# Node stage of a graph network: where GpSimd makes two low parts, and which engine casts what

## What is computed

```
h   = layernorm(x)
agg = segment_sum(relu([h[src], edge_attr] @ W1.T + b1) @ W2.T + b2, dst)
gi  = agg @ W_ih.T + b_ih ;  gh = h @ W_hh.T + b_hh
r   = sigmoid(i_r + h_r) ; z = sigmoid(i_z + h_z) ; n = tanh(i_n + r * h_n)
h_new = (1 - z) * n + z * h
x1  = x + h + batchnorm(h_new)
h2  = layernorm(x1)
top 2 of 8 gate logits -> softmax -> comb (8 numbers a node, 2 not zero)
out = x1 + sum_e comb_e * (relu(h2 @ W1_e + b1_e) @ W2_e + b2_e) + 0.5 * shared(h2)
```

## Time and profile before

| | |
|---|---|
| median of three runs | 1423.47 us |
| profiled execution | 1422.28 us, span 1420.5 us |
| TensorE busy | 1356.3 us (95%) |
| weight load busy | 1088.8 us (77%) |
| VectorE | 1030.6 us (73%) |
| GpSimd | 827.6 us (58%) |
| ScalarE | 738.2 us (52%) |
| mean granted TensorE clock | 0.991 of full speed |
| DMA | 179.57 MB, 126 GB/s over the span |

### The profile page before, as it was taken

One profiled execution on the slowest core, in us unless ns is written; L12 is line 12 of the kernel. 1 busy time (PEld: TensorE's weight loads), 2 busy tenths in 40 slices (PEclk: granted clock), 3 DMA queues, 4 the chain that ended last, 5 costly groups with the idle time before them and its releaser, 6 DMA issues.

```text
span 1420.5 us, 22825 instructions
## 1 busy us (share of the span) xinstructions
PE 1356.3 (95%) x6398; PEld 1088.8 (77%) x6398; DVE 1030.6 (73%) x2194; ACT 738.2 (52%) x1665; POOL 827.6 (58%) x1119
## 2 busy tenths in 40 slices
PE   4889999999889999999999999999999999999996
PEld 3668888887668777877787778777777777777774
DVE  3586444233478888888888888888888888888885
ACT  3431323212466566656665666566666666666552
POOL 3210242103477777777777777777777777777771
PEclk9999999999989999999999999999999999999997
DMA  8222534246423333333333333333333333333330
GB/s 311 69 68 88 185 135 144 90 152 244 163 97 126 119 132 112 127 116 133 113 129 112 133 118 125 111 133 118 125 111 133 119 124 112 131 122 122 114 109 30
DMA packets 62863, 179.57 MB, mean 126 GB/s; under 512 B 9328, under 2 KB 9968, under 8 KB 62704
## 3 DMA queue, kind: packets, MB, share of 16 engines
q1 hardware_dynamic: 46912, 99.20, 20.4%
q0 software_dynamic: 15920, 79.97, 16.4%
HBM read 141.86 MB, written 37.29 MB: 126 GB/s over the span
## 4 chain that ended last, share of the span: by engine, by line
PE 89%; DVE 4%; issue 2%; DMA 1%; ACT 1%; POOL 1%; POOLq 0%; SPq 0%; DVEq 0%; ACTq 0%
PE bank L1547 45%; PE bank L1584 9%; PE bank L1214 8%; PE bank L1594 8%; PE bank L526 6%; PE bank L1166 5%; PE bank L1184 4%; PE bank L1197 3%; PE bank L1596 1%; POOL whh_lo_raw L766 1%; PE bank L1148 1%; DVE st_e L890 1%; DMA late_out<-gates_in,carry_at 1%; DMA whh_lo_raw<-in_whh_t 0%; DVE found L957 0%
## 5 line engine op out<-in xcount | busy, mean ns | idle before, releaser
L1547 PE MATMUL bank<-whh_hi,x_hi 128*128 128x512 f32 x948 | 382.5, 403 | 10.8 <-DVE x L1493 10.5
L1547 PE MATMUL bank<-whh_hi,x_lo 128*128 128x512 f32 x948 | 375.3, 396 | 0.0
L1547 PE MATMUL bank<-whh_lo,x_hi 128*128 128x512 f32 x948 | 375.2, 396 | 0.0
L1547 PEld LDWEIGHTS bank<-whh_hi,x_hi 128*128 128x128 f32 x948 | 178.5, 188 | 51.6 <-DVE x L1493 10.9
L1547 PEld LDWEIGHTS bank<-whh_hi,x_lo 128*128 128x128 f32 x948 | 178.4, 188 | 43.5
L1547 PEld LDWEIGHTS bank<-whh_lo,x_hi 128*128 128x128 f32 x948 | 178.7, 189 | 39.1
L1295 POOL TENSOR_TENSOR rstd<-var_eps,minus_half 128x1 f32<-128x1 f32 x158 | 90.6, 574 | 149.5 <-DVE var_eps L479 149.5
L1346 POOL TENSOR_TENSOR h_n<-h,n_gate 128x512 f32<-128x512 f32 x79 | 103.9, 1315 | 58.6 <-ACT n_gate L1402 58.6
L504 ACT ACTIVATE h<-xt,shift,rstd 128x512 f32<-128x512 f32 x79 | 64.5, 816 | 134.1 <-POOL one_rstd L1301 134.1
L1286 POOL DMA_INDIRECT gates<-gates_in,slot_at x79 | 85.3, 1079 | 60.0 <-issue 45.7
L1342 POOL TENSOR_TENSOR n_pre<-r_hn,gates 128x512 f32<-128x512 f32 x79 | 102.6, 1299 | 13.4 <-POOL r_hn L1338 13.2
(11 more groups left out here) (184 smaller groups left out, 3148.6 us busy)
## 6 DMA issues: line engine op xcount, KB each, us to landing
xt<-in_x SPq DMA_DIRECT2D x79, 256.0 KB, 2.9
x_lo_raw<-in_x_cols SPq DMA_DIRECT2D x79, 256.0 KB, 2.7
out<-y SPq DMA_DIRECT2D x79, 256.0 KB, 2.0
gates_in<-g_out SPq DMA_DIRECT2D x16, 768.0 KB, 4.0
wih_lo_raw<-in_wih_t SPq DMA_DIRECT2D x4, 768.0 KB, 15.7
whh_rows<-in_whh SPq DMA_DIRECT2D x4, 768.0 KB
whh_lo_raw<-in_whh_t SPq DMA_DIRECT2D x4, 768.0 KB, 7.5
gates_in<-late_out SPq DMA_DIRECT2D x6, 256.0 KB, 6.8
```

Of the source, the lines that this page charges most:

```text
L1547: last = pe.matmul(to[0:R, :], a[:, s, k * R:(k + 1) * R], w[:, k, q * D:(q + 1) * D], start=n == 0, stop=n == 3 * DK - 1)
```

## The change

Three engines' orders change in the node stage, and one instruction goes from VectorE to ScalarE. On GpSimd the extras' low part of tile t-2 goes from behind the slot copy to right behind the second norm, and `x_low` of tile t+1 from behind `x_h_b` to between n_pre and the wait for tanh. On ScalarE the extras' cast goes from behind the r gate's sigmoid to ahead of the second norm's rows. The cast of the expert numbers leaves VectorE, and ScalarE does it after its wait for `top_i_done`, ahead of the shared expert's relu, with one more wait for the weight products of the tile before.

```diff
 # GpSimd
                 if p.has(-1):
                     norm(p, -1, 2)
+                if p.has(-2):
+                    s = p.slot(-2)
+                    pool.wait_ge(extra_hi_done, t - 1)
+                    pool.tensor_tensor(hid[:, s, HE + 2 * V:HE + 3 * V], extra[:, :], hid[:, s, HE:HE + V],
+                                       ALU.subtract).then_inc(extra_lo_done, 1)
                 if p.has(1):
...
-                if p.has(1) and not p.early(1):
-                    x_low(pool, p)
                 if p.has(2) and not p.early(2):
                     pool.wait_ge(gates_loaded[p.slot(0)], 16 * (p.turn(0) + 1))
                     slots(p, 2)
-                if p.has(-2):
-                    s = p.slot(-2)
-                    pool.wait_ge(extra_hi_done, t - 1)
-                    pool.tensor_tensor(hid[:, s, HE + 2 * V:HE + 3 * V], extra[:, :], hid[:, s, HE:HE + V],
-                                       ALU.subtract).then_inc(extra_lo_done, 1)
...
                     pool.tensor_tensor(n_pre[:, :], r_hn[:, :], gates[:, s, 2 * D:G3], ALU.add).then_inc(n_pre_done, 1)
+                if p.has(1) and not p.early(1):
+                    x_low(pool, p)
+                if p.has(0):
+                    s = p.slot(0)
                     pool.wait_ge(n_done, t + 1)
 # ScalarE
                 if p.has(2) and not p.early(2):
                     first_norm(act, p)
+                if p.has(-2):
+                    s = p.slot(-2)
+                    act.wait_ge(comb_done, t - 1)
+                    wait_from(act, hid_turned, t - 3)
+                    act.activation(hid[:, s, HE:HE + 2 * V].bitcast(F32R).rearrange("p (q v) -> p q v", q=2),
+                                   extra[:, :].unsqueeze(1).broadcast_to((R, 2, V)), ACT.Copy).then_inc(extra_hi_done, 1)
                 if p.has(-1):
...
-                if p.has(-2):
-                    s = p.slot(-2)
-                    act.wait_ge(comb_done, t - 1)
-                    wait_from(act, hid_turned, t - 3)
-                    act.activation(hid[:, s, HE:HE + 2 * V].bitcast(F32R).rearrange("p (q v) -> p q v", q=2),
-                                   extra[:, :].unsqueeze(1).broadcast_to((R, 2, V)), ACT.Copy).then_inc(extra_hi_done, 1)
...
                     act.wait_ge(top_i_done, t)
+                    wait_from(act, comb2_done, t - 1)
+                    act.activation(top_f[:, :], top_i[:, 0:2], ACT.Copy).then_inc(top_f_done, 1)
 # VectorE
                     dve.max_index(top_i[:, :], top[:, :], f1[:, 0:NE]).then_inc(top_i_done, 1)
-                    dve.wait_ge(top_i_done, t)
-                    dve.tensor_copy(top_f[:, :], top_i[:, 0:2]).then_inc(top_f_done, 1)
```

## The result

The changed kernel takes 1388.41 us (median of 4 runs, 1387.63 to 1388.83) against 1422.61 (4 runs): ratio 0.976, 95% interval 0.9747 to 0.9772. It was forecast at 1395 with a range from 1390 to 1412. The direction came as written, and so did the way there (GpSimd's ring falls under TensorE's length, and TensorE becomes the bound). The profiled execution took 1388.83 us (span 1387.0).

What follows compares the result with a forecast made beforehand. GpSimd's queue with VectorE's chain was taken as the bound at 12.88 us a tile; falling to 12.34 it leaves TensorE's 12.52. 76 x 0.36 = 27.4 plus 0.5 for ends off 1422.28 gave 1395, range 1390 to 1412.

Steps and rivals of the forecast that it cites:

- The bound: GpSimd's queue and VectorE's chain set the 12.88 us tile; TensorE alone could do 12.52, second by 0.36.
- x_lo in the wait for tanh: On GpSimd, x's low part (1.30) moved behind n_pre covers the idle wait for tanh: 0.75 us off a tile's period.
- The new wait for the cast: GpSimd's early extras subtraction waits for ScalarE's cast: 0.21 us a tile added, between 0.1 and 0.6.
- The ring: GpSimd and VectorE's loop from h_n to h_n: -0.75 + 0.21 = -0.54, from 12.88 to 12.34 us a tile.
- VectorE's cast: The expert numbers' cast, 1.09 us on VectorE, is a wait for GpSimd's h_n; removing it gives 0 to 0.03 a tile.
- The time won at TensorE: TensorE's late transposes stop waiting, 0.29 at hid and 0.07 at h2: 0.36 us a tile, 27.4 over 76 tiles.
- the ends: First and last tiles outside the steady stretch: -0.5 us in all, between -1.5 and +0.3.
- A: Rival: GpSimd's loop stays the bound through a longer cast wait and late r_gate; 12.70 a tile, 1409 us; chance 0.17.
- B: Rival: hid's gap on TensorE isn't from the extras' low part and stays; 5.3 us off, 1418; chance 0.04.
- C: Rival: VectorE's gap subtraction waits for GpSimd's h_n; 12.64 a tile, 18.2 us off, 1405; chance 0.04.
- D: Rival, slower: x_lo on GpSimd is stretched in its new place; with 0.93 more, 13.27 a tile, 1453 us; chance 0.06.

Runs made afterwards that it cites:

- run 5: The kernel before the change with 6 of TensorE's 55 matmuls a tile left out: 1419.12 us against 1421.53, ratio 0.9984.
- run 2: The kernel before with only the extras' cast on ScalarE and subtraction on GpSimd moved to the head: 1439.14 us, ratio 1.0115.
- run 6: The changed kernel with 6 of TensorE's 55 matmuls a tile left out: 1376.98 us, period 12.31.
- Run 3: The changed kernel with the expert numbers' cast back on VectorE: 1389.31 us, ratio 0.9768.
- Runs 1: The kernel before with only x's low part moved behind n_pre on GpSimd: 1400.0 us against 1422.95, ratio 0.9841.
- run 10: The changed kernel with GpSimd's extras subtraction back behind the slot copy and 6 of TensorE's 55 matmuls a tile left out: 1372.8 us.
- run 7: The changed kernel with hid's transposes right behind those of h2, ahead of the z gate's second half: 1388.06 us, ratio 0.9769.
- 8: The changed kernel with hid's transposes right behind those of h2 and GpSimd's extras subtraction back behind the slot copy: 1389.19 us.
- run 9: The changed kernel with only GpSimd's extras subtraction back behind the slot copy: 1388.17 us, ratio 0.976.
- run 4: The changed kernel with ScalarE's cast of the extras back behind the r gate's sigmoid: 1502.84 us, ratio 1.0563.

## Why the prediction was right in kind and short in size

- **The bound.** "GpSimd together with VectorE's chain; TensorE is second by 0.36". Shown: run 5 (TensorE's work cut by 1.0 a tile, 0.02 won) and run 2 (TensorE's visible wait removed, slower). Against the 12.44 that it reached, TensorE was second by 0.44.
- **x_lo in the wait for tanh.** 0.75 off the ring. The 0.74 of idle time is gone, x_lo kept its 1.30.
- **The new wait for the cast.** 0.21 summed, 0.21 in the tile shown, from start to start.
- **The ring, 12.34.** Run 6 measured 12.31.
- **VectorE's cast**, said to be a wait and worth 0 to 0.03 a tile. Run 3: 0.17 us long once h_n is out of its way, no time won by its removal.
- **The time won at TensorE: this is the step that failed**, as a size. The prediction took the two starts that were late, 0.29 at hid and 0.07 at h2; the table has 0.284 and, without the start-up value, 0.08. But it set "TensorE alone could do a tile in 12.52", where the runs show 12.44, and left the turns themselves at the length that they had while TensorE was late. A turn that isn't late is shorter: h2's by 0.058, hid's by 0.033, of which 0.013 is lost again in the matmuls behind. That is 0.078 a tile, 76 x 0.078 = 5.9 of the 6.3 us that were missing. (The medians differ by 34.2, the two profiled spans by 33.5.) Runs 1 and 2 separate the two turns: there hid's is free and takes 0.249 and 0.246, and h2's is late and takes 0.412 in both, as in the kernel before. The trace had shown half of it: in the last tile with gates hid's turn took 0.24 to f1 and not 0.27. The prediction read the start from those rows and not the length. The matmul behind hid's turn (1391.98 in the earlier trace rows) in that tile:

```profile
1392.22 0.38 PE L1584 MATMUL bank<-f_hi,h_hi 128*128 128x296 f32 x1
```

- **The range.** Below the forecast the sum had nothing but the ends: 1395.5 with -1.5 for them in place of -0.5 is 1394.5. The rest of the way down to 1390 was margin without a term, and less than the 5.9 that the turns gave. Since the ring (12.31) lay below TensorE's true 12.44, the whole of the error came through.
- **Rivals.** None came. A: the wait stayed at 0.21, and what is next to be late at r_hn is hn (run 10), not r_gate. B: hid's gap went. C: the gap subtraction stayed at 0.21. D: x_lo stayed at 1.30.

Neither run 7 nor 8 beats the changed kernel; run 9 equals it with one move less.

## What to carry to other kernels

Where every engine works in order, follow the period as a ring (here h_n to h_n) and fill the idle slot that lies in it with work that is needed late; a wait seen on the busiest engine may be only the slack of that ring, and removing its cause can cost time. Before an instruction is put at the head of a queue, its producer must come before all that stands there on the other engine too: the same order of GpSimd gave -34 us with the cast early and +80 with it late. When an engine's stall is to go, take the length of what follows it from a place without the stall, since the start that is late is not all of the loss.

## What the runs showed of the hardware beyond what was expected

- A turn's weight load started with the matmul in front where its data was there (710.08 after), and only at the turn where it wasn't (707.67 before). Four transposes then took 0.41 and not 0.35 us to the next matmul, three 0.28 and not 0.25.
- VectorE's cast of two integers a row took 0.17 us beside GpSimd's rstd (128x1, run 3) and 1.09 where it met h_n (128x512, before).
- Seven transposes in a row cost no less than four and three with matmuls between (12.43 and 12.44 a tile): one starts 0.109 behind another, but a matmul only 0.028 behind the last of a group.
- From the end of a 128x512 operation on VectorE (hn) to GpSimd's start it was 0.144 to 0.150 us wherever GpSimd waited for it (runs 9 and 10), from ScalarE to GpSimd 0.08.
- From the end of GpSimd's subtraction to hid's turn it was 0.25 us before, but from the end of x_lo to the first gate matmul 0.07 in run 4, where TensorE waited for it. So the 0.25 is not what every crossing from GpSimd to TensorE costs; what else is in it stays open.
